# Attention kernel: both norms' sums of squares as one plain fp32 product each, instead of two reduced products over squares split in high and low parts

## What is computed

```python
def _layer_norm(x, g, b):
    mu = jnp.mean(x, axis=-1, keepdims=True)
    var = jnp.var(x, axis=-1, keepdims=True)
    return (x - mu) * jax.lax.rsqrt(var + EPS) * g + b
...
shortcut = x
h = _layer_norm(x, ln1_g, ln1_b)
h = jnp.roll(h, (-SHIFT, -SHIFT), axis=(1, 2))
xw = _window_partition(h, WS).reshape(-1, N, C)
qkv = xw @ w_qkv + b_qkv
...
attn = jax.nn.softmax(attn.reshape(-1, HEADS, N, N), axis=-1)
o = jnp.einsum('whnm,whmd->whnd', attn, v)
...
x = shortcut + o
y = _layer_norm(x, ln2_g, ln2_b)
```

## Time and profile before

| | us |
|---|---|
| median of 3 runs | 3990.65 |
| the profiled execution, its own time | 3992.1 |
| its span in the trace | 3990.3 |
| TensorE busy | 3711.8 |
| VectorE busy | 2432.0 |
| ScalarE busy | 2334.6 |
| GpSimd busy | 2240.8 |
| mean granted TensorE clock | 0.972 |

### The profile page before, as it was taken

How to read it: one execution, slowest core, us unless ns; L and a number is a source line. 1 busy time by engine, 2 the same in 40 slices (tenths; PEclk the granted TensorE clock), 3 DMA queues, 4 the chain that set the end, 5 groups by cost and what they waited for, 6 DMA issues and landing times. The chain is left out here.

```text
span 3990.3 us, 95518 instructions
## 1 busy us (share of the span) xinstructions
PE 3711.8 (93%) x33140; PEld 2678.4 (67%) x33140; DVE 2432.0 (61%) x3923; ACT 2334.6 (59%) x4212; POOL 2240.8 (56%) x2186
## 2 busy tenths in 40 slices
PE   6889789999999999999999999959999999999999
PEld 3556566666666666666666666647777777777776
DVE  4544367777777777777777777743444434444343
ACT  3343167777777777777777777734444444444444
POOL 1111156666666666666666666635655656556564
PEclk7898899999999999999999999979999999999999
DMA  4331111111111111111111111145445454454542
GB/s 105 97 97 48 56 32 37 37 37 37 37 37 39 38 38 38 37 37 37 37 37 37 39 38 38 35 72 99 76 86 88 70 98 75 86 88 70 98 75 47
DMA packets 235743, 229.73 MB, mean 58 GB/s; under 512 B 118064, under 2 KB 230704, under 8 KB 232624
## 3 DMA queue, kind: packets, MB, share of 16 engines
q1 hardware_dynamic: 235696, 229.14, 28.2%
HBM read 151.26 MB, written 77.76 MB: 57 GB/s over the span
## 5 line engine op out<-in xcount | busy, mean ns | idle before, releaser
L1233 POOL TENSOR_TENSOR hid_lo<-hid,hid_hi 96x448 fp32r<-96x448 f32 x448 | 771.2, 1727 | 583.5 <-ACT hid_hi L1306 583.5
L613 POOL TENSOR_TENSOR kex<-ks,cw 112x294 f32<-112x294 f32 x1024 | 734.3, 752 | 232.1 <-ACT ks L865 232.1
L1303 ACT ACTIVATE hid<-ps_h,cw 96x448 f32<-96x448 f32 x448 | 324.0, 723 | 728.0 <-PE ps_h L1254 728.0
L1365 DVE SCALAR_TENSOR_TENSOR xr<-ps_f,cw,xr 48x448 f32<-48x448 f32 x224 | 151.3, 676 | 773.2 <-PE ps_f L1265 773.2
L673 PE MATMUL ps_s<-kex,qbd 112*98 112x294 f32 x2048 | 591.9, 410 | 0.0
L1250 PE MATMUL ps_h<-ya_hi,wa_hi 128*96 128x448 f32 x1344 | 501.4, 373 | 30.1 <-DVE yb_sp L1339 30.1
L1250 PE MATMUL ps_h<-ya_hi,wa_lo 128*96 128x448 f32 x1344 | 498.4, 371 | 0.0
L1250 PE MATMUL ps_h<-ya_lo,wa_hi 128*96 128x448 f32 x1344 | 498.2, 371 | 0.0
L1012 DVE TENSOR_TENSOR s<-ps_s,bias 98x294 f32<-98x294 f32 x1024 | 434.9, 454 | 14.1 <-PE ps_s L673 2.1
L673 PEld LDWEIGHTS ps_s<-kex,qbd 112*98 112x98 f32 x2048 | 318.0, 165 | 165.8 <-issue 80.2
L888 ACT ACTIVATE pt<-ps_t 98x588 f32<-98x588 f32 x512 | 338.6, 661 | 120.1 <-PE ps_t L684 114.5
(11 more groups left out here) (152 smaller groups left out, 6767.4 us busy)
## 6 DMA issues: line engine op xcount, KB each, us to landing
ya<-y_chunks SPq DMA_DIRECT2D x64, 532.9 KB, 6.4
y_chunks<-y SPq DMA_DIRECT2D x256, 76.1 KB, 1.8
xin<-x_chunks SPq DMA_DIRECT2D x256, 73.5 KB, 2.5
xres<-x_chunks SPq DMA_DIRECT2D x256, 73.5 KB, 1.9
x_chunks<-xo SPq DMA_DIRECT2D x256, 73.5 KB, 1.8
out<-xr SPq DMA_DIRECT2D x32, 588.0 KB, 8.2
yb<-y_chunks SPq DMA_DIRECT2D x96, 177.6 KB, 8.2
xr<-x_chunks SPq DMA_DIRECT2D x32, 514.5 KB, 5.6
```

What stands on the lines that cost most here:

```text
L613: pool.tensor_tensor(kex[a][:, win, :, :], ks[:, win, :].unsqueeze(1).to_broadcast([PP, HEADS, N]), w("head").unsqueeze(2).to_broadcast([P ...
L1233: pool.tensor_tensor(hid_lo[:, U % slots, :], hid[:, U % slots, :], hid_hi[:, U % slots, :], ALU.subtract).then_inc(hid_lo_set, 1)
L1303: act.activation(hid[:, U % slots, :], ps_h[U % slots][0:half, 0:T1], ACT.Gelu, bias=w("t1")[:, U % 2:U % 2 + 1], scale=w("s1")[:, U % 2:U ...
```

## The change

Both norms' squares are computed once, in fp32. ScalarE's second square (`sq_hi`, `sq2_hi`) and GpSimd's subtraction (`sq_lo`, `sq2_lo`) are gone, with their tiles and semaphores; TensorE's `variance` and `variance2` wait for the square itself and call `misc` with `w("sum")`, one plain fp32 product of 112 x 392, in the same bank and at the same place in TensorE's order. The copy `sum_r` and the wait for it are gone. Nothing else is edited.

```diff
-        sum_r = sb("sum_r", [PP, PP], F32R)
         sq = sb("sq", [PP, T2])
-        sq_hi, sq_lo = sb("sq_hi", [PP, T2], F32R), sb("sq_lo", [PP, T2], F32R)
-        sq2_hi, sq2_lo = sb("sq2_hi", [PP, T2], F32R), sb("sq2_lo", [PP, T2], F32R)
...
-            def split_squares(n):
-                pool.wait_ge(squared, n + 1)
-                pool.tensor_tensor(sq_lo[:, :], sq[:, :], sq_hi[:, :], ALU.subtract).then_inc(sq_split, 1)
-
-            def split_squares2(n):
-                pool.wait_ge(squared2, n + 1)
-                pool.tensor_tensor(sq2_lo[:, :], sq2[:, :], sq2_hi[:, :], ALU.subtract).then_inc(sq2_split, 1)
-
...
                 before2, before, after, after2 = at_edges(n)
-                if after:
-                    split_squares(n + 1)
-                if before2:
-                    split_squares2(n - 2)
                 shift(n)
...
-            split_squares(0)
             before_twice(0)
...
-            split_squares2(CHUNKS - 2)
             normalize2(CHUNKS - 2, last, 0)
-            split_squares2(CHUNKS - 1)
             normalize2(CHUNKS - 1, last, 1)
...
-            def sum_squares(bank, hi, lo, signal):
-                pe.matmul(ps_m[bank][0:PP, 0:T2], sum_r[:, :], hi[:, :], start=True, stop=False)
-                pe.matmul(ps_m[bank][0:PP, 0:T2], sum_r[:, :], lo[:, :], start=False, stop=True).then_inc(signal, 1)
-
...
             def variance(n):
-                pe.wait_ge(sq_split, n + 1)
-                sum_squares(0, sq_hi, sq_lo, var_mm)
+                pe.wait_ge(squared, n + 1)
+                misc(0, w("sum"), sq[:, :], var_mm)
...
             def variance2(n):
-                pe.wait_ge(sq2_split, n + 1)
-                sum_squares(1, sq2_hi, sq2_lo, var2_mm)
+                pe.wait_ge(squared2, n + 1)
+                misc(1, w("sum"), sq2[:, :], var2_mm)
...
             pe.wait_ge(biases, 4)
-            pe.wait_ge(sum_set, 1)
...
             def squares():
-                act.activation(sq[:, :], ps_m[0][0:PP, 0:T2], ACT.Square)
-                act.activation(sq_hi[:, :], ps_m[0][0:PP, 0:T2], ACT.Square).then_inc(squared, 1)
+                act.activation(sq[:, :], ps_m[0][0:PP, 0:T2], ACT.Square).then_inc(squared, 1)
...
-                act.activation(sq2[:, :], ps_m[1][0:PP, 0:T2], ACT.Square)
-                act.activation(sq2_hi[:, :], ps_m[1][0:PP, 0:T2], ACT.Square).then_inc(squared2, 1)
+                act.activation(sq2[:, :], ps_m[1][0:PP, 0:T2], ACT.Square).then_inc(squared2, 1)
...
-            dve.tensor_copy(sum_r[:, :], w("sum")).then_inc(sum_set, 1)
             dve.tensor_scalar(wqs[:, :], w("wq"), w("g1"), SCALE, op0=ALU.mult, op1=ALU.mult).then_inc(folded, 1)
```

More of the change, by code:

```diff
@@ L457, in attention @@
             sem("folded"), sem("bias_mm"), sem("biases"), sem("bp_mm"), sem("tables"), sem("pad_set"))
-        sum_set = sem("sum_set")
-        sq_split, sq2_split = sem("sq_split"), sem("sq2_split")
         x_in = [sem(f"at_x_in{a}") for a in range(2)]
```

## The result

The changed kernel takes 4051.11 us (median of 4 runs, 4050.59 to 4052.09) against 3990.64 us before (4 runs beside it): ratio 1.0152, 95% interval 1.0134 to 1.0169. It is slower by 60.5 us; 4062 (+71) had been forecast, with 4038 to 4076 as the range.

What follows compares the result with a forecast made beforehand. TensorE's unbroken work, then a ScalarE and GpSimd chain, was taken to bound the attention chunk. Steady +74.1 and edges -3.3 made +70.8 us on 3992.1, so 4062.9, or 4062 for the median; range 4038 to 4076.

Steps and rivals of the forecast that it cites:

- What bounds: Steady attention: TensorE unbroken from value product to end of `variance2`, then some 4.0 us of ScalarE and GpSimd.
- Norm 2, +0.31: Norm 2's sum behind the scores: plain product instead of the reduced pair costs TensorE +0.31 us per chunk.
- norm 1, +0.28: Norm 1's sum: pair takes 0.45 us, plain product 0.73, read off the query product; +0.28 us per chunk.
- The steady part, +74.1: Steady attention chunks: 35.3 us for norm 1 plus 38.8 for norm 2; removed squares and subtractions costed at nothing.
- The tie of y and L1028: GpSimd's `y` and VectorE's L1028, before the copy of `h`, arrive together; the three end about the same time: 0.
- The edges, -3.3: Attention stage's first and last chunks and prologue: removed work no longer waited for there, -3.3 us in sum.
- Rival 1: Both norms: plain product costs its second half in full, +79.5 us, or 4070; chance 0.22 together with rival 4.
- rival 3: Both norms' slots: durations are right, starts mislead; steady cost 0, only edges count, 3987, no change; chance 0.05.
- Rival 4: Queries' wait of 0.72 us grows, ScalarE late for L901; by 0.1 us gives 4074; chance 0.22 with rival 1.

Runs made afterwards that it cites:

- pair_no_split: Kernel before, keeping TensorE's four reduced products but with low parts set to zero once, plain squares and subtractions left out: 3974.43 us, ratio 0.9958.
- after_twice_plain: Changed kernel with each norm's plain product issued twice, the first result overwritten by the second: 4174.55 us, ratio 1.0465 to the kernel before.
- after_var2_first: Changed kernel with norm 2's product ahead of the third pair of windows' scores instead of behind them: 3977.78 us, ratio 0.9970 to the kernel before.
- norm1_plain: Kernel before with the change at norm 1 only, norm 2 keeping its split and pair: 4023.74 us, ratio 1.0079.

## Why the prediction was right, and where it was off

- **What bounds.** Right. What made TensorE's unbroken part longer or shorter went into the chunk: +0.30 and +0.27 for a norm, -0.18 for a reduced pass. It holds near the kernel before: doubling the plain products went in by 0.94 of 1.32 us, since the wait for the copy of `h` gave way.
- **Norm 2, +0.31, and norm 1, +0.28.** The slots, from a product's start to the next instruction's, grew by 0.31 and 0.30. Reading the start of norm 1's product off the query product (0.73) was 0.02 short of 0.75. The weight loads in the trace of the kernel before fit the reason given: those of norm 1's high part are loaded from 1515.64, when its product itself starts, those of the low part from 1515.73, 0.18 us ahead of theirs. The trace has a reduced pass at 0.18 us and a plain product at 0.66, each for 392 columns at 2.4 GHz. The Trainium skill, FP8 and Floating Point Precision, TensorE Precision Notes, says that true fp32 takes four passes. The trace agrees as far as a ratio can: 0.66 is 3.7 times 0.18.
- **The steady part, +74.1.** The chunk grew by 0.566, so 125 x 0.566 = 70.8; 3.3 us less. The slots gave 0.61; 0.035 came back on GpSimd, which I had costed at nothing (pair_no_split), and 0.01 is left. The step that failed is "in the steady chunk I cost them at nothing": it looked only at who waits for the squares, not at what stands behind the subtraction in GpSimd's list.
- **The tie of y and L1028.** Right, to 0.06 us, and its price too: the copy, last of the three, ended 2.02 us after the start of `y`, as before. after_twice_plain shows the other side of it. The Trainium skill, GPSIMD Engine Reference, section 1 Specifications, says that GpSimd shares its SBUF interfaces with VectorE, with contention for VectorE instructions that have two SBUF inputs. L1028 is one such, and stretches from 0.77 to 1.58 us under `y`; the bias addition (L984), with one input in PSUM, takes 0.82 us for two under the copy (1516.38), which is as short as it gets anywhere in the stage's steady part.
- **The edges, -3.3.** Mis-sized. The stage grew by 63.2 where 125 chunks at 0.566 make 70.8, so the edges gave 7.6. At its start the prologue is 0.3 us shorter and the first three steps from chunk to chunk (starts of norm 1's centering) 1.7, 0.55 and 0.3 us, so 2.8 in all where I had 1.6 (chunk 2 was counted as steady). The edge terms of the prediction add up to 3.2, not 3.3. At the end I had costed norm 2's last product but one at the slow clock. These are the rows of the kernel before there:

```profile
2606.86 0.67 PE L718 MATMUL ps_m<-sq_hi,sum_r 112*112 112x392 f32 x1 [1.93 <-POOL sq_lo L590]
...
2607.78 2.19 PE L699 MATMUL ps_o<-vs,pt 98*49 98x18 f32 x48
```

Before, TensorE was idle 1.93 us and then ran at the lower level, 1.2 GHz (granted clock 0.50 from 2607.8 to 2610.0): 2.19 us for the 48 value products. In the changed kernel it was idle 0.46 us and stayed at 2.4 GHz (1.00 in the stretch from 2670.8 to 2673.0 in the windows rows above): 1.28 us for the same (2671.58). From the last chunk but one's residual to the end of the stage it is 20.2 us before and 15.6 after, 4.6 us where I had 1.6.
- **Rival 1** (full pass at both norms, 4070) did not come, **rival 3** (no change) neither: the starts of the rows told the cost, not the durations. **Rival 4**: the queries' wait shrank by 0.05 us instead of growing.
- **The total.** +70.8 forecast, +63.2 in the stage, +60.5 in the medians. What lies between the last two is in stages that weren't touched. The +70.8 was 10.3 us too high: 3.3 in the steady part, 4.3 in the edges, 2.7 outside the stage. All three err the same way, so none hid another.

## What to carry to other kernels

Before trading a split into reduced parts for one plain fp32 product, ask which engine sets the pace: here a norm's pair cost TensorE 0.35 to 0.45 us and two engines with time to spare another 1.4, the plain product cost TensorE 0.66 to 0.75, and TensorE was the bound. Read a matmul's price as the distance from its start to the next start, between neighbours of the same kind.
A change that shortens a latency is worth something only if the order of work uses it. The same plain product was 60 us slower at its old place and 11 us faster than the kernel before one place earlier. That is no case for the plain product: the split with both moves is 26 us faster than the plain product with both. Compare two forms each at its best order. And the cheapest gain of all, 49 us, was a copy that stood behind a product that it did not need.

## What the runs showed of the hardware that had not been expected

- Two instructions on GpSimd and one on VectorE with two SBUF inputs drag each other out: the copy of `h` takes 0.51 us when VectorE's subtraction is already past, and 1.06 us when it isn't; the subtraction itself 0.77 alone, 1.33 with 0.31 us of lag behind `y`, 1.58 with 0.06. It looks like taking turns. In the medians of the steady chunks it started anywhere from 0.03 us after `y` (the changed kernel, 1.61 us long) to 0.63 (after_var2_first, 1.02 us long), and ended 1.64 to 1.65 us after `y` had started each time, and `y` kept its 1.02. Yet `y`, subtraction and copy take 2.02 us together, and 1.02 + 0.77 + 0.51 = 2.30 by themselves, so some 0.14 us of each that waits is overlapped.
- The eight value products take 0.85 us to the next start after an idle wait, 0.78 without one, so 0.07 us more.
- TensorE's granted clock fell after 1.93 us of idle time at the end of the stage, and did not after 0.46. But the length of the idle time doesn't settle it: in norm1_plain the clock fell one set of value products earlier, after 1.30 us idle (the 48 products at 2631.31 took 2.19 us, granted clock 0.50 from 2631.3 to 2633.5), and the kernel before had the same 1.30 us idle at that place and stayed at 2.4 GHz (1.28 us at 2599.09). Of the 4 us that norm1_plain takes more there, 3.2 lie between these value products and the next 48 (11.89 us, in the kernel before 8.69). What decides is not told apart here.
- Whether a subtraction stands in GpSimd's list goes with a shift of a later instruction by some 0.06 us in every second chunk, though GpSimd is idle for over 1.6 us in between. The cause stays open.
